# A selective-scan layer and a linear-attention layer on one core: split scans at unit 8, and an earlier x projection and output on TensorE

## The chip, the cores and the metric

One NeuronCore of one Trainium2 chip runs the whole kernel. The metric is the device time of one execution in microseconds (us), lower is better.

Names: PE is TensorE (PEld its weight loads), DVE is VectorE, ACT is ScalarE, POOL is GpSimd, SP is SyncE, whose queue issues the DMAs. A line number such as L1000 is a line of the kernel before.

## What is computed

For 8 batches of 256 tokens with 256 features, in float32, two layers follow each other. The first is a Mamba block with a modulated layer norm, the second a linear attention with softmax over features (q) and over tokens (k). Cut to what matters:

```python
# layer 0, per batch
xn = layernorm(x) * (1 + scale) + shift            # shift, scale, gate from silu(cond)
x_in, z = split(xn @ in_proj_w.T)                  # 512 + 512 channels
u = silu(causal_conv4(x_in) + conv_b)
dt_r, B, C = split(u @ x_proj_w.T)                 # 64, 16, 16: "x projection"
dt = softplus(dt_r @ dt_proj_w.T + dt_proj_b)
h[t] = h[t-1] * exp(dt[t] * A) + dt[t] * u[t] * B[t]     # 512 channels x 16 states
y = (sum over the 16 states of h * C + u * D_param) * silu(z)
x1 = x + gate * (y @ out_proj_w.T)
# layer 1, per batch
q, k, v = projections of layernorm(x1); softmax(q), softmax(k), mask
y = q @ (k.T @ v)
out = x1 + silu(layernorm(y) * (1 + scale2) + shift2) @ W_out + b_out
```

## The kernel before, in words

**Units.** The scan is cut into units. A batch has U = 16 of them: 4 blocks of 128 channels (`dc`) times 4 groups of 4 states (`q`). Unit g belongs to batch g // 16 and has index i = g % 16. There are 128 units in all, and every engine's program is one loop over g, from -26 on, with the batch's other steps hung on a slot: a step with slot s runs for batch b at g = 16 b + s, after the work of unit g itself. `due` and `due_by` work out the batch. So steps of four batches lie side by side: slots up to -1 prepare the batch that comes next, slots 17 and more finish batches before. Below, "index" means g % 16.

**What each engine does for one unit.**
- ACT, `decays` (L766): four exponentials of 256 columns each into one half of `ring` (a PSUM buffer of two units, four planes each), one plane for each state. Only the last of the four raises `s_da_ready`. It has to wait until DVE has done with the unit two before.
- POOL, `inputs_of` (L545): dt*u times the broadcast B rows (`Br`) into `hs`, a ring of 10 units.
- DVE, `scan_unit`: it waits for `s_da_ready` and for POOL's inputs, runs one scan over 1024 columns (L1000) and multiplies with C (`Cr`, L1012), which raises `s_hc_dve`. In four of the 16 units (indices 1, 5, 9, 13) POOL does that product (L554) instead.
- PE, `sum_states` (L1370): eight transposing matmuls that add the states of the unit up in the PSUM tile `YT`. The sums of a unit whose product is POOL's follow those of the next unit; so at index 6 PE does units 6 and 5, 16 matmuls. After every fourth unit DVE multiplies `YT` with silu(z) in `gate_y` (L1019), which waits for `s_y_acc`, the count of units summed. At index 8 it stands behind unit 8's scan and product and needs the sums of unit 7, the eighth unit of the batch.

**Steps around index 6 to 12.** In the order of each engine's program:
- ACT, index 7, behind unit 7's exponentials: `silus` (L885), with one table load ahead and one behind it. It makes silu(z) and u of the batch that comes next and the silu of batch b-2's last step (the input of `output`). Unit 8's exponentials come only behind it. Index 9: `normalize1`. Index 10: `copy_xdbl` (the result of the x projection, from PSUM to `xdbl`), `norm1`, `finish` (the output of the attention layer to SBUF). Index 11: `softplus_parts_0`.
- PE, index 7, behind unit 7's sums: `output` (one bias matmul, L1432, eight matmuls L1437, four L1517; these are for the batch two before the one whose scan runs, which is b-3 counted from the batch that is being prepared), then `x_proj` (eight matmuls, L1323), then `transpose_x1`. Index 8, behind unit 8's sums: `dt_proj_0`, then `q_and_k`.
- SP: when `copy_xdbl` is done, xdbl's B and C rows go to DRAM and come back as broadcasts, each group as soon as its last reader is done (`broadcast_bc`); behind these in the same queue stand the store of an output, a load of x and one of the gate.

**Buffers on PE's side.** `x_proj` needs u and the silu of z (whose second half is read from the same PSUM tile, PX). `output` needs the silu of step `silu_h` and PY, which `gate_x` (index 5) has read. Batches 2 to 7 have an `output` in their index 7; batches 0 to 6 have an `x_proj` there. The last batch has neither x projection nor silu of u.

Of the kernel before, what the change touches and what calls it, by code (L numbers as in the profile page):

```python
# [15 lines left out]
ALU = mybir.AluOpType  # L16
# [11 lines left out]
NQ = 4  # L28
UPC = N // NQ
U = DC * UPC  # L30
# [4 lines left out]
DBUF, XBUF = 10, 4  # L35
# [24 lines left out]
def due(g, slot):  # L60

    b, at = divmod(g - slot, U)
    return b if at == 0 and 0 <= b < NB else None


def by_pool(g):

    return g % U in (1, 5, 9, 13) and g > 1


def pool_units(g):
# [4 lines left out]
def dve_units(g):  # L76
    return g - pool_units(g)
# [33 lines left out]
def build(nc, a, out):  # L111
    ctx = ExitStack()
    with ctx:
        def sb(name, shape):
            return ctx.enter_context(nc.sbuf_tensor(name, shape, F32))
# [4 lines left out]
        def ps(name, shape):  # L120
            return ctx.enter_context(nc.psum_tensor(name, shape, F32))

        def sem(name):
            return ctx.enter_context(nc.semaphore(name))
# [38 lines left out]
        Br, Cr = sb("Br", [P, N, T]), sb("Cr", [P, N, T])  # L163
        hs = sb("hs", [P, DBUF, NQ, T])
# [24 lines left out]
        ring = ps("ring", [P, 2, NQ, T])  # L189
# [63 lines left out]
        s_dtu_ready = sem("dtu_ready")  # L253
        s_dt_ready = sem("dt_ready")
        s_da_ready = sem("da_ready")
        s_dbu_first = sem("dbu_first")
        s_dbu_ready = sem("dbu_ready")
        s_scan_done = sem("scan_done")
        s_hc_dve = sem("hc_dve")
# [47 lines left out]
        b_loaded, c_loaded = [sem(f"b_loaded{q}") for q in range(UPC)], [sem(f"c_loaded{q}") for q in range(UPC)]  # L307
# [290 lines left out]
        def _(act):  # L598
# [127 lines left out]
            def softplus_second():  # L726
                act.wait_ge(s_vabs_ready, 1)
                nc.scalar.activation(vln[:, 1], vln[:, 1], ACT.Exp, scale=-1.0).then_inc(s_vexp_ready, 1)
                act.wait_ge(s_vexp_ready, 1)
                nc.scalar.activation(vln[:, 1], vln[:, 1], ACT.Ln, bias=1.0).then_inc(s_vln_ready, 1)  # L730
# [15 lines left out]
            def decays(b, i):  # L746

                g, dc, q = U * b + i, i // UPC, i % UPC
                if g == 0:
                    act.wait_ge(s_first_dt, 1)  # L750
                elif g == UPC:
                    act.wait_ge(s_dt_ready, 1)
                elif i % (U // 2) == 0:
                    act.wait_ge(s_dt_ready, 2 * b + i // (U // 2) + 1)
                if g == 0:
                    act.wait_ge(s_aneg_ready, 1)
                if g == 1:
                    act.wait_ge(s_dbu_first, 1)
                if g >= 2:
                    if by_pool(g - 2):  # L760
                        act.wait_ge(s_scan_done, g - 1)
                    else:
                        act.wait_ge(s_hc_dve, dve_units(g - 1))
                for j in range(NQ):
                    c = N * dc + NQ * q + j
                    ins = nc.scalar.activation(ring[:, g % 2, j, :], dt[:, b % 2, dc, :], ACT.Exp,  # L766
                                               scale=Aneg[:, c:c + 1])
                ins.then_inc(s_da_ready, 1)

            def copy_yg(b):  # L770
# [131 lines left out]
            for g in range(FIRST, NB * U):  # L902
                if 0 <= g < NB * U:
                    decays(g // U, g % U)
                if g == 0:
                    softplus_parts(0, 1)
                if g == 1:
                    softplus_second()
                for dc in range(DC):
                    b = due(g, UPC * dc - 2)  # L910
                    if b is not None:
                        skip_term(b, dc)
                if g == LAST_B * U + 14:
                    last_yg((2,), PX)
                for slot, step in ((34, moments2), (-17, normalize0), (-16, modulated), (-15, conv_last_tap_0), (-14, conv_last_tap_1),
                                   (-11, copy_z), (-6, copy_xdbl), (-5, softplus_parts_0), (-3, softplus_parts_1),
                                   (19, copy_yg), (25, normalize1), (26, norm1), (30, exp_q), (30, exp_k), (31, mask_v), (32, copy_qT),
                                   (33, copy_kT), (36, normalize2), (42, finish), (-29, moments0)):
                    late = 2 if step in (conv_last_tap_0, conv_last_tap_1) else 1 if step is modulated else 0
                    b = due_soon(g, slot) if step is normalize0 else due_by(g, slot, late)  # L920
                    if (b, step) == (0, softplus_parts_1):
                        continue
                    if b is not None:
                        step(b)
                if g == 2:
                    softplus_log(0, 1)
                if g == LAST_B * U + 13:
                    last_yg((0, 1), PX)
                if (g + 9) % U == 0 and 0 <= (g + 9) // U < NB + 3:
                    silus((g + 9) // U)  # L930
# [4 lines left out]
        def _(dve):  # L935
            V = nc.vector
# [53 lines left out]
            def scan_unit(b, i):  # L990
                g = U * b + i
                q = i % UPC
                dve.wait_ge(s_da_ready, g + 1)
                if g == 0:
                    dve.wait_ge(s_dbu_first, 1)
                else:
                    dve.wait_ge(s_dbu_ready, g)
                driven = hs[:, g % DBUF].rearrange("p n t -> p (n t)")
                decays = ring[:, g % 2].rearrange("p n t -> p (n t)")
                V.tensor_tensor_scan(driven if by_pool(g) else decays, decays, driven, 0.0, ALU.mult, ALU.add).then_inc(  # L1000
                    s_scan_done, 1)
                if by_pool(g):
                    return
                dve.wait_ge(s_scan_done, g + 1)
                if i < 2 * UPC:
                    dve.wait_ge(c_loaded[q], 16 * (b + 1))
                if g == NB * U - 1:
                    for half, done in ((slice(0, 2), s_last_half), (slice(2, NQ), s_hc_dve)):
                        V.tensor_tensor(hs[:, g % DBUF, half], ring[:, g % 2, half], Cr[:, NQ * q:NQ * q + NQ, :][:, half],
                                        ALU.mult).then_inc(done, 1)  # L1010
                    return
                V.tensor_tensor(hs[:, g % DBUF], ring[:, g % 2], Cr[:, NQ * q:NQ * q + NQ, :], ALU.mult).then_inc(s_hc_dve, 1)  # L1012
# [184 lines left out]
            for g in range(FIRST, NB * U):  # L1197
# [7 lines left out]
                for dc in range(DC):  # L1205
                    b = due(g, UPC * (dc + 1))
                    if b is not None:
                        gate_y(b, dc)
                for slot, step in ((-25, stats0), (-16, conv_taps_0), (-14, conv_taps_1), (21, gate_x),
                                   (22, stats1), (27, max_qk), (30, sum_k), (32, head_blocks), (33, normalize_q),  # L1210
                                   (34, stats2)):
                    b = due_by(g, slot, 3 if step in (conv_taps_0, conv_taps_1) else 0)
# [11 lines left out]
        def _(pe):  # L1224
# [392 lines left out]
            for g in range(FIRST, NB * U):  # L1617
                b = due(g, 19)
                if b is not None:
                    out_proj(b)  # L1620
                if 0 <= g < NB * U and not by_pool(g):
                    sum_states(g // U, g % U)
                    if summed_after(g) is not None:
                        sum_states(summed_after(g) // U, summed_after(g) % U)
                if g == LAST_B * U + 12:
                    pe.wait_ge(s_last_yg, 2)
                    last_back((2,), PX, 3)
                for slot, step in ((17, transpose_back), (-19, transpose_x), (-18, in_proj_0), (-16, in_proj_1), (-14, in_proj_2),
                                   (-13, in_proj_3), (39, output), (-9, x_proj), (-8, dt_proj_0), (-6, dt_proj_1),
                                   (23, transpose_x1), (24, q_and_k),  # L1630
                                   (28, v_rows), (29, transpose_qk), (31, k_times_v), (31, q_times_att),
                                   (35, transpose_y)):
                    b = due_by(g, slot, -2 if step is in_proj_1 else 2 if step in (in_proj_2, in_proj_3) else 0)
                    if b is not None and not (b == LAST_B - 1 and step in (k_times_v, q_times_att)):
                        step(b)
                if g == LAST_B * U + 10:
                    pe.wait_ge(s_vabs_ready, 2 * NB)
                    last_back((0, 1), PX, 2)
                if g == LAST_B * U + 13:
                    last_early(1)  # L1640
                if g == LAST_B * U + 14:
                    last_early(0)
                if g == -2:
                    setup_emb()
# [40 lines left out]
```

## Time and profile before

| what | value |
|---|---|
| runs of the kernel before | 556.62, 561.06, 560.0 us; median 560.0 us |
| the profiled execution | 559.76 us, span 558.0 us |
| busy share of the span | DVE 90%, POOL 81%, PE 79%, ACT 77%, PEld 65% |
| busy time | DVE 504.7 us, POOL 449.6 us, PE 438.2 us, ACT 430.8 us |
| mean granted TensorE clock | 0.887 |

The span runs from the first to the last instruction; some 1.8 us of the execution's own time lie outside it. In a timeline row the numbers are start and duration in us, then engine, line, operation, output and input; a bracket at the end is idle time of the engine just before, with the instruction that released it. A row with xN holds N instructions that followed each other.

### The profile page before, as it was taken

How to read it: one execution, taken by the hardware profiler on the slowest of the kernel's cores; microseconds unless marked ns; L12 is line 12 of the kernel's file. 1: busy time of each engine (PE TensorE's matmuls, PEld its weight loads, DVE VectorE, ACT ScalarE, POOL GpSimd, SP SyncE). 2: the span in 40 equal slices, each digit the busy share in tenths (PEclk: the TensorE clock that was granted, in tenths of full speed). 3: DMA queues.
4: the chain of work that ended last, by engine and by line, in shares of the span. 5: the costliest groups of instructions: out<-in, count | busy, mean ns of one | idle time of the engine just before them, and what ended most of it. 6: DMA issues, size and time to landing. Idle time of an engine off the chain costs nothing. (4 is left out here: it accounts for less than half of the span.)

```text
span 558.0 us, 7398 instructions
## 1 busy us (share of the span) xinstructions
PE 438.2 (79%) x2438; PEld 364.5 (65%) x2438; DVE 504.7 (90%) x520; ACT 430.8 (77%) x992; POOL 449.6 (81%) x306
## 2 busy tenths in 40 slices
PE   8968756769688788779788678769677878959797
PEld 7657445557576677657676667658565766847675
DVE  2489899999999989999999999999999988999853
ACT  2694868689879989798979989799877797686444
POOL 4059979989997989979997999979997979995121
PEclk8978868887899698998899899989899697779899
DMA  8295043102330144011430044003320044000001
GB/s 250 90 330 150 0 140 97 68 23 77 120 114 2 28 153 170 3 28 52 152 122 0 29 156 168 0 11 117 122 85 9 2 165 159 1 0 20 1 1 38
DMA packets 22366, 45.38 MB, mean 81 GB/s; under 512 B 3684, under 2 KB 13556, under 8 KB 22328
## 3 DMA queue, kind: packets, MB, share of 16 engines
q1 hardware_dynamic: 22328, 44.92, 24.6%
q8 instruction: 19, 0.31, 0.2%
q14 instruction: 19, 0.16, 0.1%
HBM read 42.52 MB, written 2.39 MB: 80 GB/s over the span
## 5 line engine op out<-in xcount | busy, mean ns | idle before, releaser
L545 POOL TENSOR_TENSOR hs<-dtu,Br 128x1024 f32<-128x1024 f32 x127 | 296.8, 2360 | 7.9 <-DMA Br<-bc_rows 6.9
L766 ACT ACTIVATE ring<-dt,Aneg 128x256 f32<-128x256 f32 x512 | 212.7, 464 | 44.0 <-DVE hs L1012 39.1
L1000 DVE TENSOR_TENSOR_SCAN ring<-ring,hs 128x1024 f32<-128x1024 f32 x97 | 221.6, 2284 | 10.9 <-ACT ring L766 10.9
L1370 PE MATMUL sums<-ident,hs 128*128 128x128 f32 x1024 | 154.9, 309 | 49.4 <-DVE hs L1012 49.3
L1370 PEld LDWEIGHTS sums<-ident,hs 128*128 128x128 f32 x1024 | 138.6, 162 | 60.6 <-DVE hs L1012 57.5
L1012 DVE TENSOR_TENSOR hs<-ring,Cr 128x1024 f32<-128x1024 f32 x96 | 117.5, 1224 | 3.3
L554 POOL TENSOR_TENSOR hs<-hs,Cr 128x1024 f32<-128x1024 f32 x31 | 73.0, 2356 | 38.7 <-DVE hs L1000 38.7
L1000 DVE TENSOR_TENSOR_SCAN hs<-ring,hs 128x1024 f32<-128x1024 f32 x31 | 70.3, 2268 | 0.0
L1437 PE MATMUL PY<-wqkvo,xT 128*128 128x256 f32 x168 | 48.3, 439 | 0.0
L1437 PEld LDWEIGHTS PY<-wqkvo,xT 128*128 128x128 f32 x168 | 39.6, 236 | 7.7
L1363 PE MATMUL sums<-ident,uD 128*128 128x128 f32 x64 | 14.3, 310 | 32.3 <-DVE ygT L1019 32.3
L962 DVE SCALAR_TENSOR_TENSOR conv<-PX,par,conv 128x255 f32<-128x255 f32 (+2 forms) x84 | 33.9, 470 | 5.3 <-ACT conv L656 5.3
L1300 PE MATMUL PX<-xnT,win 128*128 128x256 f32 x112 | 30.8, 423 | 3.5 <-ACT xnT L647 2.5
L1363 PEld LDWEIGHTS sums<-ident,uD 128*128 128x128 f32 x64 | 8.3, 158 | 35.5 <-DVE hs L1012 35.0
L1300 PEld LDWEIGHTS PX<-xnT,win 128*128 128x128 f32 x112 | 22.7, 213 | 8.0 <-ACT xnT L647 3.7
L1305 PE MATMUL PX<-win,xnT 128*128 128x512 f32 x52 | 25.5, 613 | 2.2 <-DVE conv L962 2.2
L1421 PE MATMUL PY<-wo,yg 128*128 128x256 f32 x112 | 25.3, 379 | 0.0
L1421 PEld LDWEIGHTS PY<-wo,yg 128*128 128x128 f32 x112 | 21.2, 190 | 5.4 <-issue 2.9
L516 POOL TENSOR_TENSOR dt<-dt,conv 128x512 f32<-128x512 f32 x15 | 19.2, 1278 | 5.3 <-ACT conv L737 4.3
L612 ACT ACTIVATE xh<-qe 128x256 f32<-128x256 f32 x12 | 4.9, 408 | 23.9 <-DVE qe L1068 23.9
L519 POOL TENSOR_TENSOR dtu<-dt,u 128x512 f32<-128x512 f32 x15 | 19.1, 1273 | 1.2
L1342 PE MATMUL PX<-xdbl,wdt 97*128 97x256 f32 x64 | 18.6, 416 | 1.4 <-ACT xdbl L696 0.7
(232 smaller groups left out, 681.7 us busy)
## 6 DMA issues: line engine op xcount, KB each, us to landing
Br<-bc_rows SPq DMA_DIRECT2D x32, 512.0 KB, 5.3
Cr<-bc_rows SPq DMA_DIRECT2D x32, 512.0 KB, 4.0
xg<-in_x SPq DMA_DIRECT2D x8, 256.0 KB, 3.0
out<-fin SPq DMA_DIRECT2D x7, 256.0 KB, 4.3
hs<-in_ada_wT SPq DMA_DIRECT2D x3, 512.0 KB, 5.1
win<-in_in_wT SPq DMA_DIRECT2D x2, 512.0 KB, 6.9
hs<-in_W_emb SPq DMA_DIRECT2D x2, 512.0 KB
gate<-gate_rows SPq DMA_DIRECT2D x8, 128.0 KB, 3.1
```

The lines of the kernel that those rows point to most:

```text
L545: nc.gpsimd.tensor_tensor(hs[:, g % DBUF], dtu[:, b % 2, dc, :].unsqueeze(1).to_broadcast([P, NQ, T]), Br[:, NQ * q:NQ * q + NQ, :], ALU.m ...
L554: nc.gpsimd.tensor_tensor(hs[:, g % DBUF], hs[:, g % DBUF], Cr[:, NQ * q:NQ * q + NQ, :], ALU.mult).then_inc(s_hc_pool, 1)
L766: ins = nc.scalar.activation(ring[:, g % 2, j, :], dt[:, b % 2, dc, :], ACT.Exp, scale=Aneg[:, c:c + 1])
L962: V.scalar_tensor_tensor(conv[:, dc, s:], xz_bank(b, h)[:, e, 0:T - s], w, conv[:, dc, s:], ALU.mult, ALU.add).then_inc(s_tap_done, 1)
L1000: V.tensor_tensor_scan(driven if by_pool(g) else decays, decays, driven, 0.0, ALU.mult, ALU.add).then_inc(s_scan_done, 1)
L1012: V.tensor_tensor(hs[:, g % DBUF], ring[:, g % 2], Cr[:, NQ * q:NQ * q + NQ, :], ALU.mult).then_inc(s_hc_dve, 1)
L1300: ins = M(xz_bank(b, h)[:, e, :], win[:, k, lo:lo + P], xnT[:, k, :], start=(k == 0), stop=(k == KD - 1))
L1305: ins = M(flat(xz_bank(b, h)), xnT[:, k, P * c:P * c + P], win[:, k, DI:2 * DI], start=(k == 0), stop=(k == KD - 1))
L1363: ins = M(YT[:, c, :], uD[:, dc % 2, P * c:P * c + P], ident[:, :], is_transpose=True, start=(c == 0), stop=False, skip_group_check=True)
L1370: ins = M(YT[:, c, :], hs[:, g % DBUF, j, P * c:P * c + P], ident[:, :], is_transpose=True, start=False, stop=(q == UPC - 1 and j == NQ - ...
L1421: ins = M(dst, yg[:, k, P * c:P * c + P], wo[:, k, :], start=(k == 0), stop=(k == DC - 1))
L1437: ins = M(dst, xT_of(b)[:, k, P * c:P * c + P], wqkvo[:, w, k, :], start=False, stop=(k == KD - 1), skip_group_check=True)
```

## The change

- `in_halves(g)` is true for unit 0 and for each unit with index 8. In these, ACT raises a new semaphore `s_da_half` after the second of four exponentials. DVE waits for it, scans planes 0 and 1 (512 columns), waits for `s_da_ready`, scans planes 2 and 3, and then does the one product as before.
- ACT: `copy_xdbl` goes from index 10 to index 8 (slot -6 to -8), and within index 10 `finish` now stands ahead of `norm1`.
- PE: `x_proj` goes from index 7 to index 6, and stands ahead of `output` there; `output` goes from index 7 to index 6 (slot 39 to 38); `dt_proj_0` goes from index 8 to index 7. So x projection and output, which stood behind the sums of unit 7, stand between the sums of units 6 and 5 and those of unit 7.

```diff
+def in_halves(g):
+    return g == 0 or g % U == 8
+
+def halves_until(g):
+    return sum(in_halves(i) for i in range(g + 1))
...
                     ins = nc.scalar.activation(ring[:, g % 2, j, :], dt[:, b % 2, dc, :], ACT.Exp,
                                                scale=Aneg[:, c:c + 1])
+                    if j == 1 and in_halves(g):
+                        ins.then_inc(s_da_half, 1)
                 ins.then_inc(s_da_ready, 1)
...
-                                   (-11, copy_z), (-6, copy_xdbl), (-5, softplus_parts_0), (-3, softplus_parts_1),
-                                   (19, copy_yg), (25, normalize1), (26, norm1), (30, exp_q), (30, exp_k), (31, mask_v), (32, copy_qT),
-                                   (33, copy_kT), (36, normalize2), (42, finish), (-29, moments0)):
+                                   (-11, copy_z), (-8, copy_xdbl), (42, finish), (26, norm1), (-5, softplus_parts_0), (-3, softplus_parts_1),
+                                   (19, copy_yg), (25, normalize1), (30, exp_q), (30, exp_k), (31, mask_v), (32, copy_qT),
+                                   (33, copy_kT), (36, normalize2), (-29, moments0)):
...
-                dve.wait_ge(s_da_ready, g + 1)
+                if in_halves(g):
+                    dve.wait_ge(s_da_half, halves_until(g))
+                else:
+                    dve.wait_ge(s_da_ready, g + 1)
...
+                if in_halves(g):
+                    first, second = (slice(0, 2), slice(2, NQ))
+                    for half in (first, second):
+                        if half is second:
+                            dve.wait_ge(s_da_ready, g + 1)
+                        a_half, x_half = (t[:, half].rearrange("p n t -> p (n t)") for t in (ring[:, g % 2], hs[:, g % DBUF]))
+                        ins = V.tensor_tensor_scan(a_half, a_half, x_half, 0.0, ALU.mult, ALU.add)
+                    ins.then_inc(s_scan_done, 1)
+                    dve.wait_ge(s_scan_done, g + 1)
+                    dve.wait_ge(c_loaded[q], 16 * (b + 1))
+                    V.tensor_tensor(hs[:, g % DBUF], ring[:, g % 2], Cr[:, NQ * q:NQ * q + NQ, :], ALU.mult).then_inc(s_hc_dve, 1)
+                    return
...
-                                   (-13, in_proj_3), (39, output), (-9, x_proj), (-8, dt_proj_0), (-6, dt_proj_1),
+                                   (-13, in_proj_3), (-10, x_proj), (38, output), (-9, dt_proj_0), (-6, dt_proj_1),
```

## Rows read from the trace of the kernel before

**Rows 1.** Waits of DVE: who waited for whom, total us, times, longest us

```profile
DVE ring L1000 <- ACT ring L766: 10.9, 14, 1.6
DVE ygT L1019 <- PE sums L1370: 0.8, 1, 0.8
```

**Rows 2.** Timeline of DVE in batch 4: products of units 6 and 7, unit 8, gate_y

```profile
309.07 1.23 DVE L1012 TENSOR_TENSOR hs<-ring,Cr 128x1024 f32<-128x1024 f32 x1
...
313.45 1.23 DVE L1012 TENSOR_TENSOR hs<-ring,Cr 128x1024 f32<-128x1024 f32 x1
315.25 2.30 DVE L1000 TENSOR_TENSOR_SCAN ring<-ring,hs 128x1024 f32<-128x1024 f32 x1 [0.58 <-ACT ring L766]
317.59 1.23 DVE L1012 TENSOR_TENSOR hs<-ring,Cr 128x1024 f32<-128x1024 f32 x1
318.73 0.41 DVE L1019 TENSOR_TENSOR ygT<-sums,zs 128x256 f32<-128x256 f32 x1
```

**Rows 3.** Timeline of ACT in batch 4: exponentials of units 8 and 9

```profile
313.55 3.27 ACT L766 ACTIVATE ring<-dt,Aneg 128x256 f32<-128x256 f32 x8
```

**Rows 4.** Timeline of DVE: its waits for exponentials at index 8

```profile
68.64 2.30 DVE L1000 TENSOR_TENSOR_SCAN ring<-ring,hs 128x1024 f32<-128x1024 f32 x1 [1.33 <-ACT ring L766]
...
189.54 2.30 DVE L1000 TENSOR_TENSOR_SCAN ring<-ring,hs 128x1024 f32<-128x1024 f32 x1 [0.58 <-ACT ring L766]
...
438.60 2.30 DVE L1000 TENSOR_TENSOR_SCAN ring<-ring,hs 128x1024 f32<-128x1024 f32 x1 [0.58 <-ACT ring L766]
```

**Rows 5.** Timeline of DVE: its waits for exponentials at index 11

```profile
200.63 2.30 DVE L1000 TENSOR_TENSOR_SCAN ring<-ring,hs 128x1024 f32<-128x1024 f32 x1 [1.55 <-ACT ring L766]
...
263.02 2.30 DVE L1000 TENSOR_TENSOR_SCAN ring<-ring,hs 128x1024 f32<-128x1024 f32 x1 [0.63 <-ACT ring L766]
...
449.74 2.30 DVE L1000 TENSOR_TENSOR_SCAN ring<-ring,hs 128x1024 f32<-128x1024 f32 x1 [1.61 <-ACT ring L766]
...
509.43 2.30 DVE L1000 TENSOR_TENSOR_SCAN ring<-ring,hs 128x1024 f32<-128x1024 f32 x1 [0.58 <-ACT ring L766]
```

**Rows 6.** Timeline of ACT in batch 2: copy_xdbl

```profile
197.09 0.38 ACT L696 ACTIVATE xdbl<-PX 96x256 f32<-96x256 f32 x1 [1.86 <-PE PX L1323]
```

**Rows 7.** Timeline of PE in batch 4: sums 6 and 5, sums 7, output, x_proj, sums 8

```profile
310.35 3.45 PE L1370 MATMUL sums<-ident,hs 128*128 128x128 f32 x16 [3.68 <-DVE hs L1012]
314.73 1.09 PE L1370 MATMUL sums<-ident,hs 128*128 128x128 f32 x8 [0.93 <-DVE hs L1012]
315.66 0.38 PE L1432 MATMUL PY<-rows,ones 97*128 97x512 bf16 x1
...
318.47 1.89 PE L1323 MATMUL PX<-u,wxp 128*96 128x256 f32 x8
...
320.85 1.04 PE L1370 MATMUL sums<-ident,hs 128*128 128x128 f32 x8
321.72 1.03 PE L1342 MATMUL PX<-xdbl,wdt 97*128 97x256 f32 x4
```

**Rows 8.** Timeline of PE in batch 1: x_proj at half clock

```profile
129.79 3.25 PE L1323 MATMUL PX<-u,wxp 128*96 128x256 f32 x8
```

**Rows 9.** Windows: stretch, length, busy us of each engine, PEclk, DMA share, GB/s

```profile
310.02:313.44 3.42, 3.10 (x15) 3.10 (x16) 3.36 (x6) 3.40 (x5) 3.42 (x2) 0.50 0.37 115
...
183.73:193.97 10.24, 8.62 (x32) 7.50 (x33) 9.56 (x11) 9.21 (x19) 9.91 (x9) 0.50 0.17 38
248.59:255.41 6.82, 5.55 (x25) 4.82 (x23) 6.17 (x6) 6.79 (x14) 6.49 (x7) 0.50 0.22 57
```

**Rows 10.** Groups of DVE: the product in one piece and in halves

```profile
L1012 DVE TENSOR_TENSOR hs<-ring,Cr 128x1024 f32<-128x1024 f32 x96 | 117.5, 1224 | 3.3
...
L1009 DVE TENSOR_TENSOR hs<-ring,Cr 128x512 f32<-128x512 f32 x2 | 1.3, 686 | 0.0
```

**Rows 11.** Timeline of the start: POOL's product and DVE's addition beside it

```profile
38.20 2.36 POOL L545 TENSOR_TENSOR hs<-dtu,Br 128x1024 f32<-128x1024 f32 x1 [0.18 <-DMA Br<-bc_rows]
...
38.88 1.95 DVE L984 TENSOR_TENSOR dt<-dt,conv 128x256 f32<-128x256 f32 x1
```

More of the change, by code:

```diff
@@ L255, in build @@
         s_da_ready = sem("da_ready")
+        s_da_half = sem("da_half")
         s_dbu_first = sem("dbu_first")
```

## The prediction

> **What bounds the kernel now.** I read the page first: DVE is busy for 90% of the span, ahead of POOL with 81%. The list of DVE's waits says what the missing tenth is: through the steady part it waits for nothing but the exponentials of ACT, 10.9 us in 14 times, and for PE's sums it waits once, 0.8 us, at the very end [rows 1]. In steady state the instructions of DVE even overlap a little: the product ends at 318.82 and its successor starts at 318.73, 0.09 us earlier [rows 2]. So DVE is the bound, its queue is strictly in order, and a wait that is taken from it or given to it counts in full. The timeline puts the waits at two places. At index 8, behind the silus, DVE waits 1.33 us in batch 0 and five times 0.58 us or 0.57 in batches 2 to 6 (first and last shown), and not at all in batches 1 and 7 [rows 4]. At index 11 it waits 1.55, 0.63, 1.61 and 0.58 us in batches 2, 3, 6 and 7 [rows 5]. The others (the start, units 6 and 115, the last one) have no part in the change. The cause at index 11 stands on ACT: copy_xdbl waited 1.86 us for the x projection [rows 6], which PE reached late because output and sums ran at half clock.
>
> I count from the end of unit 6's product, "P". In batch 4, P is 309.07 + 1.23 = 310.30 [rows 2].
>
> **The split scan.** Unit 8's exponentials start at 313.55 and take 3.27 / 8 = 0.41 us each [rows 3]; two are done at about 314.4, and DVE is free at 313.45 + 1.23 = 314.68 [rows 2]. So the first half never waits, and the second, needed over 1.1 us later, finds its exponentials done at 315.2. Each of the five waits goes, with 0.09 us of lost overlap: 5 x 0.67 = 3.3 us. In batch 0 the wait is 1.33 us and the half signal comes two exponentials earlier, 0.82 us [rows 3, 4]: gain 0.8. The cost is one more DVE instruction in eight units. No trace row shows a scan of 512 columns; the product shows what a cut costs: 2 x 0.686 - 1.224 = 0.15 us [rows 10], less 0.09 if the halves overlap as others do [rows 2]. I take 0.11, from 0.06 to 0.15. In seven units that is 0.8 us. Unit 0 counts as nothing: two instructions behind it DVE adds dt in 1.95 us, an operation of a quarter of a product's size, and it ends 0.27 us after POOL's product, which was started by a DMA at 38.20 and ends at 40.56 [rows 11]. If DVE comes half a microsecond earlier, it still ends where POOL ends; whatever unit 0 gains is given back there. If that cover is not real, 0.5 us more are won. The Trainium skill says the same of such a pair (SBUF — State Buffer, "SBUF: two separate sides"): a VectorE instruction with two SBUF inputs and a GpSimd one exclude each other for the whole instruction. By a reading without that lock the sum would be lower by that half microsecond.
>
> **The waits at index 11.** With x_proj ahead of output and of unit 7's sums, and copy_xdbl moved to index 8, nothing at index 10 of ACT waits for PE any longer, and in batch 7, where norm1 stood behind PE's output, that is done earlier too. I let all four go: 1.55 + 0.63 + 1.61 + 0.58 + 4 x 0.09 = 4.7 us [rows 5]. The B and C broadcasts on SP's queue, and the store, the load and the gate behind them, start up to two units earlier; POOL and DVE don't wait for them in the steady part, so that is worth nothing, and the loads still wait for their buffers' readers. finish ahead of norm1 costs norm1 one copy, some 0.5 us, on ACT, which has already given up copy_xdbl's 0.38 us there [rows 6]; nothing.
>
> **What the new order on PE costs.** This is the added wait. PE's queue is in order, and unit 7's sums now stand behind x_proj and output. DVE's gate_y behind unit 8 needs these sums, and everything of DVE is queued behind gate_y. The chain at full clock, from P:
> - 0.05 us to PE's start [rows 2, 7]
> - 16 sums: eight take 1.04 us and the next group starts after 0.87 [rows 7], so 1.74
> - x_proj 1.89 less the same 0.17 of overlap: 1.72 [rows 7]
> - output from 315.66 to 318.47: 2.81 [rows 7]
> - unit 7's sums 1.04, and 0.05 back to DVE.
>
> That is 7.41 us. u and the silus that both steps need are made before PE reaches them, in ACT's silus ahead of 313.55 [rows 3]. If L us of the chain lie at half clock, it is 7.41 + L/2. DVE's own arrival at gate_y, if nothing holds it: unit 8 starts at 314.68 - 0.09 = 314.59, gate_y follows 318.73 - 315.25 = 3.48 us later [rows 2], and the cut adds 0.11: 318.18, or P + 7.88. So the new wait is S = L/2 - 0.47.
>
> L decides. PE comes out of 3.68 us of idleness here [rows 7], and the granted clock is 0.50 (the 1.2 GHz level) around P in every batch from 1 to 7. It went back to 1.00 after stretches of three lengths [rows 9]: 3.42 us (3.14 behind P, batch 4; batch 5 alike), 6.82 us (batch 3), 10.24 us (batch 2, 9.4 behind P; batches 1, 6 and 7 alike). In the long ones PE stood idle once more, 0.7 to 1.3 us ahead of unit 7's sums; in batch 4 that gap was 0.93 [rows 7], but came when the clock was back. The new order fills this gap, so I don't expect the 9.4. I take L between 3.1 and 6.4 (6.82 less what lies ahead of P), middle 4.7: S = 1.9 us. Ends for the range: L = 3.1 gives 1.1 us, L = 6.4 gives 2.7; L = 9.4 would give 4.2, and full clock throughout none. Five batches (2 to 6) have both steps: 5 x 1.9 = 9.4 us (4.7 x 0.5 - 0.47 = 1.88 each).
>
> The Trainium skill (TensorE: Matmul & The Clock Gate, "What's actually happening") states that "the default state is throttled, and activity releases the throttle". Rows 9 agree, and by that rule the filled gap ends the slow stretches earlier.
>
> Batch 7 has output alone: 7.41 - 1.72 + 4.7/2 = 8.04 against 7.88, so 0.2 us (0 to 1.0). Batches 0 and 1 have x_proj alone: 7.41 - 2.81 + L/2 is under 7.88 for any L up to 6.4, so gate_y doesn't wait. But copy_xdbl now stands between the exponentials of units 8 and 9. In batch 1 x_proj at half clock takes 3.25 us [rows 8], starts some 3.5 after P and ends at 6.7, while ACT asks at about P + 4.9 (four exponentials after 313.55, [rows 3]). Units 9's and 10's exponentials come later by that, and there is 0 to 0.6 us for DVE; I take 0.4. In batches 2 to 6 the same delay lies under the wait at gate_y.
>
> **The sum.** Gains: 3.3 + 0.8 + 4.7 = 8.8. Costs: 0.8 + 9.4 + 0.2 + 0.4 = 10.8. Net 2.0 us longer: 559.76 + 2.0 = 561.8 for the profiled execution. The median of the runs shown is 0.24 us above that execution, so I say 562.0.
>
> **Rivals.**
> - *The sums come in time and DVE gains* (8%). PE then has slack that I don't see, or the clock is full: S = 0, and the net is -8.8 + 0.8 = -8.0, 552 us. For it: gate_y never waited for the sums in steady state [rows 1]. Against: these sums stood first in line then; and half clock at P is in all seven batches.
> - *Short half clock* (20%). L about 3 or less in all five batches: S = 0.5 to 1.1, costs 0.8 + 2.5 to 5.5, net -5.5 to -2.5: 554.5 to 557.5 us. For it: batches 4 and 5.
> - *Long half clock: the wait at gate_y overtakes all gains* (14%). This is the one on the other side: the place is gate_y at index 8 of batches 2 to 6, behind x_proj and output. From S = 1.5 us, that is L = 4.0, it makes the kernel slower than before. With L = 9.4, as four of seven batches had, S is 4.2 and the net is -8.8 + 1.4 + 21 = +13.6, 574 us; with half of the batches so, 568. For it: four of seven batches. Against: they had the gap.
> - The forecast itself has 58%, with L of 3.5 to 6.4 in the mean.
>
> **How the numbers follow.** The forecast's own range is S of 1.3 to 2.7 in five batches and the bounds of the cut, 558.5 to 566.5. To reach 8 in 10 I take in most of the short case and the lower part of the long one: 555.5 to 568. About 1% is what a measurement of this kernel can tell from no change (554.4 to 565.6): faster 0.12 (the first rival and a little of the second), slower 0.20 (the long case and the end of the forecast), the same 0.68.
>
> **What would show it.** In the profile after: no wait of DVE for exponentials at index 8 and 11 (the list drops from 10.9 to some 3 us); a new entry, gate_y L1019 of before waiting for PE's sums, five times, 5 to 13 us in all; on PE, x_proj and output between the 16 sums and the 8 sums without a gap; the half-clock stretches behind P no longer than 6.9 us; unit 0's scan starts half a microsecond earlier and unit 2's no earlier than before. If gate_y doesn't wait, or waits over 3 us each time, the step on L or on the chain is wrong. If the waits at index 11 stay, the step on copy_xdbl is.

## The result and the profile after

Twelve runs of the kernel after took 557.58 to 564.2 us, median 562.81; twelve of the kernel before 556.62 to 562.38, median 558.04. The ratio is 1.0081 (95% interval 1.0056 to 1.0106): 4.5 us longer, 0.8%, with the interval from 3.1 to 5.9. The forecast was 562.0, 2.0 us longer than the median of 560.0 that the three known runs of before had. The profiled execution after took 561.79 us with a span of 560.0, also 2.0 longer than the profiled execution of before. That this agrees to the digit is luck, as the accounts below show: the change itself cost more than twice what was forecast. Where runs of one kernel lie more than 1.5% above its fastest, its ratio leaves them out: of the kernel before in the set of experiments 5 to 8 that leaves 21 runs of 35 with a median of 557.03 us (all 35 have 559.66), and three runs of kernel 1 and two of kernel 9, all near 563 us, stand outside theirs.

The waits of DVE in the profile after (who waited for whom, total us, times, longest):

```profile
DVE ygT L1046 <- PE sums L1397: 12.1, 8, 2.5
...
DVE ring L1027 <- ACT ring L776: 1.7, 3, 0.9
...
DVE att L1084 <- PE PZ L1518: 0.6, 1, 0.6
DVE ring L1019 <- ACT ring L776: 0.5, 1, 0.5
```

Against [rows 1] the two entries have changed places: DVE waited 10.9 us for exponentials and 0.8 for sums, now 2.2 and 12.1. No wait at index 11 is left, none at index 8 but that of batch 0. The new one is gate_y, now L1046. DVE, PE and ACT in batch 2 (product of unit 6, product of unit 7, the two half scans as one row, product of unit 8, gate_y; then the steps of the other two):

```profile
183.22 1.22 DVE L1039 TENSOR_TENSOR hs<-ring,Cr 128x1024 f32<-128x1024 f32 x1
...
187.60 1.23 DVE L1039 TENSOR_TENSOR hs<-ring,Cr 128x1024 f32<-128x1024 f32 x1
188.75 2.34 DVE L1019 TENSOR_TENSOR_SCAN ring<-ring,hs 128x512 f32<-128x512 f32 x2
191.12 1.23 DVE L1023 TENSOR_TENSOR hs<-ring,Cr 128x1024 f32<-128x1024 f32 x1
194.66 0.42 DVE L1046 TENSOR_TENSOR ygT<-sums,zs 128x256 f32<-128x256 f32 x1 [2.32 <-PE sums L1397]
```

```profile
184.50 3.68 PE L1397 MATMUL sums<-ident,hs 128*128 128x128 f32 x16 [3.56 <-DVE hs L1039]
187.97 2.97 PE L1350 MATMUL PX<-u,wxp 128*96 128x256 f32 x8
190.78 0.38 PE L1459 MATMUL PY<-rows,ones 97*128 97x512 bf16 x1
...
193.59 1.04 PE L1397 MATMUL sums<-ident,hs 128*128 128x128 f32 x8
```

```profile
190.98 0.38 ACT L706 ACTIVATE xdbl<-PX 96x256 f32<-96x256 f32 x1 [1.60 <-PE PX L1350]
```

Unit 7's product ends at 188.83, and its sums start at 193.59, behind x_proj and output without a gap between them: this is the wait that was forecast. ACT now waits for x_proj at index 8, as forecast under the cover of gate_y's wait. The half scan starts 0.08 us ahead of the end of the product before it, so its exponentials never hold it.

The waits at gate_y of batches 3 to 6 (that of batch 2, 2.32 us, stands above), and then the half-clock stretch behind each sixth product of the five batches (windows: stretch, length, busy us of PE, PEld, DVE, ACT, POOL, granted clock, DMA share, GB/s):

```profile
257.05 0.42 DVE L1046 TENSOR_TENSOR ygT<-sums,zs 128x256 f32<-128x256 f32 x1 [1.24 <-PE sums L1397]
320.74 0.42 DVE L1046 TENSOR_TENSOR ygT<-sums,zs 128x256 f32<-128x256 f32 x1 [2.54 <-PE sums L1397]
383.12 0.42 DVE L1046 TENSOR_TENSOR ygT<-sums,zs 128x256 f32<-128x256 f32 x1 [1.25 <-PE sums L1397]
445.23 0.42 DVE L1046 TENSOR_TENSOR ygT<-sums,zs 128x256 f32<-128x256 f32 x1 [0.96 <-PE sums L1397]
```

```profile
183.32:190.15 6.83, 5.65 (x22) 4.94 (x23) 6.76 (x9) 6.02 (x11) 6.51 (x6) 0.50 0.21 58
248.18:251.59 3.41, 3.41 (x17) 3.39 (x16) 3.34 (x6) 3.38 (x6) 3.41 (x2) 0.50 0.37 115
309.62:316.44 6.82, 6.08 (x23) 5.22 (x24) 6.75 (x9) 5.58 (x10) 6.49 (x8) 0.50 0.20 60
374.47:377.88 3.41, 3.41 (x17) 3.24 (x15) 3.34 (x5) 3.38 (x6) 3.41 (x2) 0.50 0.00 0
435.91:439.32 3.41, 2.89 (x14) 2.90 (x15) 3.38 (x6) 3.39 (x6) 3.41 (x3) 0.50 0.01 2
```

Half clock behind P (P is the sixth product's end, in batch 2 at 183.22 + 1.22 = 184.44) was 5.71 us in batch 2 (190.15 - 184.44), 3.41 in batch 3, 6.15 in batch 4, 3.41 in batch 5 and 2.96 in batch 6. The prediction's S = L/2 - 0.47 gives 2.4, 1.2, 2.6, 1.2 and 1.0; measured, with the lost overlap of 0.09, are 2.4, 1.3, 2.6, 1.3 and 1.1. No stretch there is longer than 6.83; the 10.24 of [rows 9] is gone.

**Where the 2.0 us of span come from.** The start of unit 12 was at 82.91 before and is at 80.35 after: -2.56. That has nothing to do with the change. All but 0.01 of it lies ahead of DVE's first addition of dt (29.20 us before, 26.65 after), where nothing was edited. TensorE's granted clock was at half (0.50) from 9.65 to 16.48 us in the profile before, and full up to 33.14 us in the profile after; that this made the difference is likely, not shown. From unit 12 to unit 124 it is 431.91 before and 435.81 after: +3.90. The rest up to the end adds 0.66. So without the setup the profiled execution would have been 4.6 us longer, near the 4.5 of the timed runs. That these two agree is no proof either, since the profiled execution before lies 1.7 us above the median of its runs and that of after 1.0 below.

### The profile page after: what moved, and what is told of

It reads as the page before. It is cut to its first block and busy times, and to the rows that moved or that the text cites. A ratio compares the mean times of both kernels' runs of the same rounds, so it can differ in the third digit from the quotient of the medians.

```text
span 560.0 us, 7415 instructions
## 1 busy us (share of the span) xinstructions
PE 430.6 (77%) x2438; PEld 358.3 (64%) x2438; DVE 506.4 (90%) x529; ACT 430.4 (77%) x992; POOL 449.6 (80%) x306
## 5 line engine op out<-in xcount | busy, mean ns | idle before, releaser
L1027 DVE TENSOR_TENSOR_SCAN ring<-ring,hs 128x1024 f32<-128x1024 f32 x88 | 200.9, 2282 | 1.9 <-ACT ring L776 1.7
L1039 DVE TENSOR_TENSOR hs<-ring,Cr 128x1024 f32<-128x1024 f32 x87 | 106.5, 1224 | 3.0
L1464 PE MATMUL PY<-wqkvo,xT 128*128 128x256 f32 x168 | 45.7, 421 | 0.0
L1464 PEld LDWEIGHTS PY<-wqkvo,xT 128*128 128x128 f32 x168 | 37.1, 221 | 7.0
L1448 PE MATMUL PY<-wo,yg 128*128 128x256 f32 x112 | 26.6, 393 | 0.0
L1046 DVE TENSOR_TENSOR ygT<-sums,zs 128x256 f32<-128x256 f32 x32 | 13.3, 416 | 12.2 <-PE sums L1397 12.1
L1019 DVE TENSOR_TENSOR_SCAN ring<-ring,hs 128x512 f32<-128x512 f32 x18 | 21.0, 1215 | 0.6 <-ACT ring L776 0.5
L666 ACT ACTIVATE conv<-PX,par 128x256 f32<-128x256 f32 x28 | 14.2, 557 | 7.9 <-PE PX L1327 7.7
```

What stands on the lines that cost most here:

```text
L1448: ins = M(dst, yg[:, k, P * c:P * c + P], wo[:, k, :], start=(k == 0), stop=(k == DC - 1))
L1464: ins = M(dst, xT_of(b)[:, k, P * c:P * c + P], wqkvo[:, w, k, :], start=False, stop=(k == KD - 1), skip_group_check=True)
```

## Experiments

The time from unit 12 to unit 124 in each profile, "the steady part" below, leaves the setup and the tail out. The kernels were timed in three sets, each beside the kernel before: 1 to 4 (median of before 558.48 us), 5 to 8 (559.66 for all its runs) and 9 and 10 (559.38). So kernels of different sets are best compared by their ratios; a gain "by the ratio" is the ratio turned into microseconds. The kernel after was timed in none of them; its 562.81 stands beside 558.04.

**1. The split scans alone.** Both tuples of steps as in the kernel before.

```diff
-(-8, copy_xdbl), (42, finish), (26, norm1) ... (-10, x_proj), (38, output), (-9, dt_proj_0)
+(-6, copy_xdbl) ... (26, norm1) ... (42, finish) ... (39, output), (-9, x_proj), (-8, dt_proj_0)
```

> Only the split scans of unit 0 and of the units with index 8; the orders on TensorE and ScalarE are those of the kernel before. Theory (gate_y waits because x_proj and output stand ahead of the eighth unit's sums): the five waits of 0.58 us and 0.8 us of the one in batch 0 go, seven cuts cost 0.11 us each, gate_y waits for nothing: net -3.3 us, ratio 0.994, the waits at index 11 stay. Rival (a cut of the scan costs more than it saves): 0 to +3 us, ratio 1.000 to 1.005, and the two halves together take over 2.6 us.

Measured: 557.62 us median, ratio 0.9977 (0.9944 to 1.001). Steady part 427.75, 4.2 us less than before. gate_y waits for nothing at index 8, the exponentials of index 8 hold nothing, and the waits at index 11 stay (2.20 and 1.27 us, in batches 2 and 3):

```profile
DVE ring L1027 <- ACT ring L776: 4.9, 5, 2.2
```

The cut of the scan is not dear: the rival falls, since the two halves take 2.34 us together and not over 2.6. In the timed runs the gain is smaller than forecast, and its interval reaches from -3.1 to +0.6 us.

**2. The order alone.** Scans in one piece, all orders as in the kernel after.

```diff
-if in_halves(g): ... two scans of 512 columns
+V.tensor_tensor_scan(...)   # 1024 columns, as before
```

> Only the new order (x_proj and output at index 6, copy_xdbl at index 8, finish ahead of norm1, dt_proj_0 at index 7), scans in one piece. Theory: the waits at index 11 go (-4.7 us), gate_y waits in batches 2 to 6 by 0.56 us less than with the split, some 1.2 us each (+6), batch 1 +0.4: net +1.7 us, ratio 1.003, and the waits at index 8 for exponentials stay at 0.58. Rival (the loss comes with the split): 0.99 or less.

Measured: 563.04 us, ratio 1.0087 (1.0057 to 1.0116). By the timed runs the whole loss of the change comes with the order. In the profile gate_y waits at index 8 in batches 2 to 6 for 0.47, 0.63, 0.62, 0.32 and 1.32 us, in four of the five less than in the kernel after, since DVE still comes later by its wait of 0.58 for exponentials there. The theory's sign is right and its size too small (+1.7 forecast, +4.9 measured). Where these 4.9 us lie the profile doesn't show: its steady part is 431.09, 0.8 us under that of before, and it is of an execution of 560.82 us, 2.2 under the median of its kernel.

**3. Output back behind the eighth unit's sums.**

```diff
-(-10, x_proj), (38, output), (-9, dt_proj_0)
+(-10, x_proj), (39, output), (-9, dt_proj_0)
```

> The kernel after with one step put back: output at index 7 behind the eighth unit's sums; x_proj stays ahead of them, and copy_xdbl at index 8. Theory: the chain from the sixth unit's product to the eighth unit's sums loses output's 2.81 us, is 4.6 us + L/2 and under 7.9 for any L up to 6.4: gate_y waits for nothing at index 8, all gains stay: net -7.5 us, ratio 0.986 to 0.989. Rival (the time goes into half clock elsewhere, or x_proj is the one that holds the sums): gate_y still waits at index 8, ratio 0.995 or more.

Measured: 558.49 us, ratio 1.0008 (0.9985 to 1.0031). The wait at gate_y, index 8, is gone in every batch, as the theory said, and this step alone is worth 4.3 us in the medians (562.81 to 558.49), 4.1 by the ratios. But the rest of the forecast 7.5 us isn't there. The steady part of its profile is 426.69, 5.2 under before; three of its batches take 61.05 us, DVE's own work without a wait, and one takes 63.85. There the granted clock was at half on the way to the conv taps (row 1), and at index 8 copy_xdbl waited for x_proj and made the exponentials of units 9 and 10 late (rows 2 and 3):

```profile
355.43 2.43 DVE L974 SCALAR_TENSOR_TENSOR conv<-PX,par,conv 128x255 f32<-128x255 f32 x6 [1.68 <-ACT conv L666]
...
380.12 2.29 DVE L1027 TENSOR_TENSOR_SCAN hs<-ring,hs 128x1024 f32<-128x1024 f32 x1 [0.30 <-ACT ring L776]
382.69 2.30 DVE L1027 TENSOR_TENSOR_SCAN ring<-ring,hs 128x1024 f32<-128x1024 f32 x1 [0.29 <-ACT ring L776]
```

**4. The kernel after, TensorE kept busy ahead of the sixth product.**

```diff
+                if g % U == 4 and U < g:
+                    keep_on(24)      # 24 bf16 matmuls into the unused half of the sums' tile
```

> The kernel after, with 24 more bf16 matmuls into the unused half of the sums' tile behind index 4 of each batch from 1 on, in TensorE's 3.7 us of idleness ahead of the sixth unit's product. Theory: the half clock behind that product goes, the chain is 7.4 us, gate_y waits 0 to 0.3 us: net against before -7 to -8 us, ratio 0.986 to 0.988. Rival (gate_y waits for order, whatever the clock, or the clock falls anyway): the waits of 1.0 to 2.5 us stay, ratio 1.005 to 1.01.

Measured: 554.24 us, ratio 0.9913 (0.9881 to 0.9945), so 8.6 us under the kernel after in the medians. PE in batch 2 (the added matmuls, then the same steps as above):

```profile
181.37 2.78 PE L1257 MATMUL sums<-ones 97*128 97x256 bf16 x24
185.21 1.97 PE L1397 MATMUL sums<-ident,hs 128*128 128x128 f32 x16 [1.05 <-DVE hs L1039]
187.01 1.89 PE L1350 MATMUL PX<-u,wxp 128*96 128x256 f32 x8
188.74 0.38 PE L1459 MATMUL PY<-rows,ones 97*128 97x512 bf16 x1
...
191.55 1.04 PE L1397 MATMUL sums<-ident,hs 128*128 128x128 f32 x8
```

The chain from 185.21 to the sums' end at 192.59 takes 7.38 us; 7.31 was forecast for full clock (7.41 with the two ways of 0.05). The sums end ahead of gate_y at 192.97, and it waits in no batch at index 8. So order and half clock together make the wait: with the order put back or the clock kept up it is gone. The steady part is 424.22, 7.7 under before. In the timed runs the gain against the kernel before is 4.9 us by the ratio (4.2 in the medians) where 7 to 8 were forecast.

**5. Both: output put back, and the clock kept up.** The edits of 3 and 4.

> The kernel with output put back behind the eighth unit's sums (x_proj still ahead), plus the 24 matmuls in TensorE's idleness behind index 4. Theory (the order cost is gone there already, and what kept its time at that of before is half clock at other places and on the way to copy_xdbl): DVE waits for nothing at index 8 to 11; against before -6 to -8 us, ratio 0.986 to 0.990, about the same as the kernel after with these matmuls. Rival (half clock had nothing to do with it): ratio 0.998 or more.

Measured: 553.52 us, ratio 0.9942 (0.9903 to 0.998), so 3.2 us under before by the ratio where 6 to 8 were forecast (6.1 under the median of all runs of before in its set). Steady part 424.29. Kernel 3, which differs only in those 24 matmuls of a batch, had a ratio of 1.0008 and is 5.0 us longer in the medians: half clock is what kept kernel 3 at the time of before. As forecast DVE waits for nothing at index 8 to 11. Three of its waits between units 12 and 124 are left, the largest for conv at index 2 (1.69 us).

**6. The kernel before, kept busy at the same place.** The edit of 4 in the kernel before.

> The kernel before, unchanged but for the 24 matmuls in TensorE's idleness behind index 4. Theory (the waits at index 11 came from half clock behind the sixth unit's product): they go, the five waits of 0.58 us at index 8 stay; -2 to -4.5 us, ratio 0.992 to 0.997. Rival (they come from the order of the steps and need the change): the waits at index 11 stay, ratio 1.000.

Measured: 557.22 us, ratio 1.0009 (0.9981 to 1.0038): the rival's number, and in part its reason. The steady part of the profile is 427.63, 4.3 under before; of that 1.7 is a wait in the last batch that got shorter (0.57 for 2.31), which the theory didn't speak of. Two waits at index 11 stay, of 0.84 and 0.80 us. PE in batch 5 tells why:

```profile
371.34 1.97 PE L1370 MATMUL sums<-ident,hs 128*128 128x128 f32 x16 [1.05 <-DVE hs L1012]
375.73 1.09 PE L1370 MATMUL sums<-ident,hs 128*128 128x128 f32 x8 [2.42 <-DVE hs L1012]
376.66 0.38 PE L1432 MATMUL PY<-rows,ones 97*128 97x512 bf16 x1
376.88 3.31 PE L1437 MATMUL PY<-wqkvo,xT 128*128 128x256 f32 x8
```

At full clock the 16 sums are done early, PE then stands idle for 2.42 us ahead of unit 7's sums, and the clock falls behind that: output's eight matmuls take 3.31 us for 1.89, and copy_xdbl waits again (1.14 us). In the new order x_proj fills this gap. That is a worth of the new order which the theory of this run had not counted.

**7 and 8. The best of both orders, with a second idle stretch filled.** Eight more matmuls ahead of q_times_att at index 15, into a tile that it overwrites. Kernel 7 has the old orders, kernel 8 those of kernel 3.

```diff
+                        if step is q_times_att:
+                            for i in range(8):
+                                M(PY[:, 0, :], ones3[:, 0:P], ones3[:, :], start=True, stop=True)
+                if g % U == 4 and U < g:
+                    keep_on(24)
```

> The split scans alone with the old orders, plus the 24 matmuls behind index 4 and 8 more, into PY ahead of q_times_att at index 15, where it is overwritten. Theory: with the clock kept up the new order is not needed at all: no wait of DVE at index 8, 11, nor of the conv taps at index 2; -7 to -9 us, ratio 0.984 to 0.988. Rival (the new order has a worth of its own): at least 2 us behind e8.

> As e7, but with x_proj and copy_xdbl ahead as in the kernel after, and output behind the eighth unit's sums. Theory: the same time as e7 within 1 us, ratio 0.984 to 0.988. Rival (the order has a worth of its own): 2 us ahead of e7.

Measured: both fall short of the forecast 0.984 to 0.988. Kernel 7 554.02 us, ratio 0.9947 (0.9917 to 0.9976), steady part 424.90; one wait at index 11 of 1.37 us, which the theory excludes, and one at gate_y, index 4 of the last batch, of 0.84. Kernel 8 552.48 us, ratio 0.992 (0.9889 to 0.9952), steady part 422.50: every batch from 1 to 5 takes 61.05 or 61.06 us, and from unit 12 to 124 DVE waits only for what the last batch brings (0.57 and 0.20 us). Kernel 8 beats both kernels of this case: it is 4.5 us under before by the ratio (7.2 under the median of all runs of before in its set), and its median is 10.3 us under that of after, in another set. It is 1.5 us ahead of kernel 7 in the medians and 2.4 in the steady parts, where the rival wanted 2; the intervals of the two overlap, so that the order has a worth of its own is likely, not shown.

**9. x_proj ahead of output, both behind the sums.** Split scans, ACT's order as before.

```diff
-(39, output), (-9, x_proj), (-8, dt_proj_0)
+(-9, x_proj), (39, output), (-8, dt_proj_0)
```

> The split scans with the orders of the kernel before, and one step swapped on TensorE: at index 7, behind the eighth unit's sums, x_proj stands ahead of output. Theory (the order cost is only what stands ahead of the sums): gate_y waits for nothing at index 8; copy_xdbl at index 10 no longer waits, but finish behind it can wait for output at half clock; against before -3 to -5 us, ratio 0.991 to 0.995. Rival (half clock takes the gain as in the kernel with x_proj ahead of the sums): 0.998 to 1.001.

Measured: 557.76 us, ratio 0.9962 (0.9928 to 0.9996), which is between the two. gate_y waits for nothing at index 8, and copy_xdbl no longer for x_proj. But norm1 takes over as the one that waits, since the transposes it reads stand behind output (batch 5):

```profile
384.63 1.02 ACT L805 ACTIVATE xT<-PZ,par 128x256 f32<-128x256 f32 x2 [2.51 <-PE PZ L1263]
```

DVE waits 2.04 us at index 11 of that batch and 1.53 in batch 2. So with this order the wait went to the reader of the last of these steps.

**10. Kernel 3 once more, for a second profile.**

> The kernel of e3_output_behind once more, for a second profile. Theory (its timed runs are 1 us over its first profile, and 4 to 5 us over the same kernel kept busy, because half clock falls on other steps from run to run): no wait at gate_y at index 8 again, and 2 to 6 us of waits of DVE for conv, for exponentials or for sums at other places than in the first profile. Rival (something else than waits costs the time): the sum of DVE's waits between the first and the last unit stays at that of the first profile.

Measured: 557.6 us, the one execution that was profiled. Again no wait at gate_y, index 8. From unit 12 to 124 DVE waits 5.3 us in nine times, against 4.3 in six in the first profile; the steady part is 428.93 against 426.69, 2.24 longer. Six of the nine are the same waits as before (the longest is conv's, 1.78 for 1.68), three small ones are new. These, with the overlap of 0.09 us that each new wait loses, make some 1.3 us. The other 0.9 lie in four idle stretches of 0.14 us that the first profile doesn't have, each some 0.23 with the lost overlap, too short for the bracket of a row. One is ahead of unit 36, whose scan starts 0.03 us behind its last exponential:

```profile
173.63 1.66 ACT L776 ACTIVATE ring<-dt,Aneg 128x256 f32<-128x256 f32 x4
```

```profile
173.95 1.23 DVE L1039 TENSOR_TENSOR hs<-ring,Cr 128x1024 f32<-128x1024 f32 x1
175.32 2.30 DVE L1027 TENSOR_TENSOR_SCAN ring<-ring,hs 128x1024 f32<-128x1024 f32 x1
```

So the waits do differ from run to run, but by less than the theory said (2 to 6 us at other places), and the rival falls too: waits, short ones included, make up the difference.

## Why the prediction was right or wrong

**The split scan: right, its price too high.** The five waits at index 8 are gone. Two half scans take 2.34 us together against 2.29 for one; the cut costs 0.05 us, just under the lower end of 0.06, where 0.11 was taken. In seven units that is 0.4 us less cost.

**Batch 0: right for unit 0, wrong for unit 8.** From DVE's first addition of dt to unit 12 it is 53.71 us before and 53.70 after: neither unit 0 nor unit 8 gained anything. For unit 0 this was forecast, with the cover of [rows 11] as the reason, and the profile after bears it out: counted from the first addition of dt its scan starts 0.51 us earlier, unit 2's 0.05. Between them the addition beside POOL's product came earlier, took 2.36 us for 1.95, and again ended 0.29 us behind POOL's product (0.27 before):

```profile
35.60 2.35 POOL L555 TENSOR_TENSOR hs<-dtu,Br 128x1024 f32<-128x1024 f32 x1 [0.17 <-DMA Br<-bc_rows]
35.88 2.36 DVE L996 TENSOR_TENSOR dt<-dt,conv 128x256 f32<-128x256 f32 x1
```

The step that failed is "in batch 0 ... gain 0.8": the same thing happens there a second time. Behind gate_y of index 8 stands a small tensor_scalar. The timelines of before (first fence) and after (second) show it behind the start of POOL's four products, which one row sums up:

```profile
63.87 9.30 POOL L545 TENSOR_TENSOR hs<-dtu,Br 128x1024 f32<-128x1024 f32 x4
72.66 0.54 DVE L1125 TENSOR_SCALAR m1s<-mods,par 128x8 f32<-128x8 f32 x1
```

```profile
61.30 9.31 POOL L555 TENSOR_TENSOR hs<-dtu,Br 128x1024 f32<-128x1024 f32 x4
69.33 1.31 DVE L1152 TENSOR_SCALAR m1s<-mods,par 128x8 f32<-128x8 f32 x1
```

It took 0.54 us and ended at 73.20, POOL's row at 73.17; now it takes 1.31 and ends at 70.64, POOL's at 70.61. Its like just behind takes 0.22. DVE came 0.77 us earlier and stood 0.77 us longer. This is read from rows and was not tried on its own. The Trainium skill (SBUF — State Buffer, "SBUF: two separate sides") says that a VectorE operation in a two-port mode and a GpSimd operation exclude each other for the whole instruction; the two ends, 0.03 us apart in both traces, agree. Whether this instruction runs in such a mode, no run here shows.

**The waits at index 11: right in the profile, too large for the timed runs.** All four are gone, 4.7 us. But their sum belongs to one execution. Twelve runs of before had a median 1.7 us below the profiled one, and fewer or shorter waits there are a likely cause; no profile of such a run was taken. For it speaks that of the 28 runs of before in the first set the sixteen with a mean granted clock of 0.898 or more have a median of 557.3 us, the twelve below have 560.1; the profiled one had 0.887. It also accounts for a part of what the kernel kept busy lacked, 4.2 us in the medians for 6.7 between the profiled executions: the one of before lay 1.3 us above its median in that set, the one of kernel 4 1.2 below its own.

**The new wait at gate_y: right, place, mechanism and size.** Forecast were five times 1.9 us, 9.4; measured 8.31 plus 0.45 of overlap, 8.8. L was 4.3 in the mean of the five, 4.7 had been taken. Runs 3 and 4 show the two conditions of it one by one, run 2 that the loss comes with the order. The gap ahead of unit 7's sums is filled, and behind P no stretch of 10.24 us is left. That the one comes of the other was not tried by itself; it fits that in kernel 3 batch 7, which has no x_proj, kept a gap of 0.71 us there and a stretch of 10.24.

**Batches 1 and 7.** At index 8 to 10 DVE waits in neither; 0.4 and 0.2 us had been forecast. In batch 1 copy_xdbl did wait for x_proj, 1.44 us, but DVE found its exponentials done all the same.

**What was missed: half clock at other steps.** The profile after has three waits of DVE that before had not: 1.63 us for the conv taps in batch 2, 0.24 and 2.13 us at gate_y with index 4 of batches 1 and 7; and one of 2.31 us in the last batch has shrunk to 0.57. Together +2.3 us. They sit behind work of TensorE that ran at half clock. In batch 1 it is the sixteen sums of units 18 and 17 (3.37 us for 1.97), in batch 2 in_proj, in batch 7 the sixteen sums and out_proj:

```profile
484.50 4.91 PE L1448 MATMUL PY<-wo,yg 128*128 128x256 f32 x16
...
490.32 0.42 DVE L1046 TENSOR_TENSOR ygT<-sums,zs 128x256 f32<-128x256 f32 x1 [2.13 <-PE sums L1397]
```

The same 16 matmuls take 3.62 us at full clock. The prediction summed the clock only where the change touched the order, and put every other step at nothing without a reason. In the profiles half clock lies on other steps after than before; that it is the shift of the batch that moves it there was not tried.

**The accounts.** Steady part, forecast: -3.3 - 4.7 + 0.8 + 9.4 + 0.2 + 0.4 = +2.8. Measured: -3.3 - 4.7 + 0.4 + 8.8 + 0 + 0 + 2.3 = +3.5, against +3.90 from the starts of the units. The other 0.4 us can be found in the rows: the three new waits lose an overlap of 0.09 each, and DVE stands idle for 0.15 us ahead of unit 36, too short for the list of waits, which costs 0.23 with its overlap. With batch 0 (-0.8 forecast, 0 measured) the forecast comes to +2.0, where the timed runs say 4.5: some 2.5 us too small. In the profiles that is half clock elsewhere 2.3, batch 0 0.8, the small waits 0.4 and the end behind unit 124 0.7, less 1.6 by which the cut, gate_y and batches 1 and 7 were put too high. The result lies in the range and inside 1%, and the case was the likeliest one. But two agreements are luck. The profiled execution came out at the forecast because a setup faster by 2.56 us hid the missing terms; and the forecast of 562.0 lies only 0.8 us from the median because the three known runs of before had a median of 560.0, 2.0 above that of the twelve. The rivals: the sums did not come in time, and neither the short nor the long half clock was there alone; L was 3.0 to 3.4 in three batches and about 6 in two.

## What to carry to other kernels

When a step is moved ahead on an in-order engine, write down the chain from the last release to the first instruction that the bounding engine waits for, at full and at half clock: here S = L/2 - 0.47 held within 0.1 us in five places. A gap on TensorE was not free here, though TensorE is not the bound: matmuls of no use in a 3.7 us gap were worth more (8.6 us) than the change had cost (4.5), and the filler belongs where the steps behind it are waited for. A single profile of a kernel whose clock moves about gives the terms, not the base: compare from one unit to another, leave the setup out, and hold the profiled execution against the median before adding to it.

## What was not expected of the hardware

- One scan of 1024 columns takes 2.29 us and two of 512 take 2.34 together, 0.05 more. By its durations alone (1.22 and 1.21 us) the cut would cost 0.15, as the product's do [rows 10]; the overlap of the two halves takes back the rest.
- A VectorE instruction on 8 columns took 1.31 us where its like takes 0.22, until POOL's running product ended; what DVE had gained just before was given back to 0.01 us.
- The half-clock stretches behind P in the five batches after are 3.41 or 6.83 us long, and those of before 3.42, 6.82 and 10.24.
